# A gated recurrence with a ternary feed-forward: Bm's products move to slot 7, two blocks of y to slot 6

## What is computed

```python
def step(carry, xs):
    r, state = carry
    qt, kt, vt = xs                       # kt = vt = ctx, qt = layernorm(x)
    r = decay * r + kt * vt
    retained = (qt * r).reshape(B, D)
    inp = retained @ Wi.T + bi
    gate = sigmoid(inp @ Wg.T + bg)
    blended = gate * state + (1.0 - gate) * inp
    state = tanh(blended @ A.T + inp @ Bm.T)
    out = state @ Wo.T + bo
    return (r, state), out
x = x + tanh(g_xattn) * outs
h = relu(layernorm(x) @ Wq1.T + b1)       # 256 -> 1024, Wq1, Wq2 ternary
x = x + tanh(g_ffn) * (h @ Wq2.T + b2)    # 1024 -> 256
```

## The kernel before

| slot | TensorE behind the step |
|---|---|
| 0 | hidden 0 (8 matmuls), transposes of xh1 (4), output 0 (6) |
| 1 | hidden 1, output 1 |
| 2 | hidden 2, `inp_product` (12) |
| 3 | hidden 3, y blocks 0, 1 (4 each) |
| 4 | y 2, 3, `gate_product` (12) |
| 5 | y 4, 5, transposes of xh2 (4) |
| 6 | y 6, 7, `from_inp` (12) |
| 7 | `from_rest` (12) |

## Time and profile before

### The profile page before, as it was taken

How to read it: one execution, slowest core, us unless ns; L and a number is a source line. 1 busy time by engine, 2 the same in 40 slices (tenths; PEclk the granted TensorE clock), 3 DMA queues, 4 the chain that set the end, 5 groups by cost and what they waited for, 6 DMA issues and landing times. The chain is left out here.

```text
span 317.4 us, 10191 instructions
## 1 busy us (share of the span) xinstructions
PE 304.0 (96%) x3818; PEld 278.1 (88%) x3818; DVE 283.4 (89%) x816; ACT 236.9 (75%) x556; POOL 78.5 (25%) x138
## 2 busy tenths in 40 slices
PE   7889979999999999999999999999999999999995
PEld 5767868899999999999999999999999999997784
DVE  5889899999999999999999999999999998968763
ACT  4585548787778787887877787878877777857693
POOL 2021133241231323141412313231414121141230
PEclk9999999999999999999999999999999999999999
DMA  7903405123444435251533434441514314171321
GB/s 283 404 11 101 100 35 82 58 49 50 134 69 136 66 118 84 71 113 33 134 45 132 66 132 66 127 71 59 126 32 135 45 66 66 69 101 36 68 33 66
DMA packets 19399, 29.16 MB, mean 92 GB/s; under 512 B 1840, under 2 KB 10288, under 8 KB 19120
## 3 DMA queue, kind: packets, MB, share of 16 engines
q0 software_dynamic: 8720, 8.39, 18.5%
q1 hardware_dynamic: 10224, 19.93, 17.9%
q10 hardware_dynamic: 432, 0.53, 0.5%
HBM read 16.26 MB, written 4.19 MB: 64 GB/s over the span
## 5 line engine op out<-in xcount | busy, mean ns | idle before, releaser
L467 ACT ACTIVATE state<-pre_ps,sc 128x64 f32<-128x64 f32 x128 | 40.0, 312 | 51.2 <-PE pre_ps L1077 51.0
L457 ACT ACTIVATE hid<-hid_ps,b_s 128x256 f32<-128x256 f32 x120 | 50.2, 470 | 11.4 <-PE hid_ps L1116 9.7
L1116 PE MATMUL hid_ps<-xt_lo,w_q 128*128 128x256 f16 x240 | 55.5, 272 | 0.0
L1128 PE MATMUL y_ps<-w_q,h_lo 128*128 128x256 bf16 x240 | 55.5, 272 | 0.0
L1116 PE MATMUL hid_ps<-xt_hi,w_q 128*128 128x256 f16 x240 | 55.5, 272 | 0.0
L1128 PE MATMUL y_ps<-w_q,h_hi 128*128 128x256 bf16 x240 | 55.5, 272 | 0.0
L1071 PE MATMUL pre_ps<-m_hi,a_hi 128*128 128x32 f16 x508 | 42.6, 179 | 4.5 <-DVE m_hi L681 4.3
L732 DVE TENSOR_TENSOR h_lo<-hid,h_hi 128x512 f16<-128x512 f32 x60 | 41.3, 688 | 3.1 <-ACT h_hi L463 1.4
L1071 PEld LDWEIGHTS pre_ps<-m_hi,a_hi 128*128 128x128 f16 x508 | 33.7, 96 | 10.7 <-DVE m_hi L681 6.5
L1071 PE MATMUL pre_ps<-m_hi,a_lo 128*128 128x32 f16 x508 | 41.5, 177 | 0.0
L463 ACT CAST h_hi<-hid 128x512 f16<-128x512 f32 x60 | 37.1, 619 | 1.9
(11 more groups left out here) (181 smaller groups left out, 916.5 us busy)
## 6 DMA issues: line engine op xcount, KB each, us to landing
x_norm<-x_in SPq DMA_DIRECT2D x16, 256.0 KB, 2.7
cx<-ctx_in SPq DMA_DIRECT2D x16, 256.0 KB, 3.1
x_res<-x_in SPq DMA_DIRECT2D x16, 256.0 KB, 3.3
x_res<-bo_g POOLq DMA_DIRECT2D x16, 256.0 KB, 4.8
x<-b_g POOLq DMA_DIRECT2D x15, 256.0 KB, 3.9
y_out<-y SPq DMA_DIRECT2D x15, 256.0 KB, 2.0
w_raw<-w_in SPq DMA_DIRECT2D x2, 1024.0 KB, 8.4
wsq<-wsq_in SPq DMA_DIRECT2D x3, 256.0 KB, 5.1
```

The lines of the kernel that those rows point to most:

```text
L457: last = nc.scalar.activation(hid[:, p % 2, u, :], hid_ps[p % 2][:, u * N:(u + 1) * N], ACT.Relu, bias=b1_s[:, 2 * p + u:2 * p + u + 1], s ...
L467: nc.scalar.activation(state[:, q[1] % 2, :, step_cols(j)], pre_ps[q[1] % 2][:, :].rearrange("p (k n) -> p k n", k=K)[:, :, step_cols(j)], ...
L1116: last = nc.tensor.matmul(hid_ps[p % 2][:, u * N:(u + 1) * N], w1_q[:, k, cut], v[:, par, k, :], start=n == 0, stop=n == len(terms) - 1)
L1128: last = nc.tensor.matmul(y_ps[:, t * D:(t + 1) * D], h[:, f, t * P:(t + 1) * P], w2_q[:, f, :], start=f == 0 and t == 0 and h is h_hi, st ...
```

## The change

Three places in TensorE's list are edited; no other engine's program changes. y's blocks 2 and 3 leave slot 4 (with the wait that they had in body 2) and go to the head of slot 6's list, so that the order of the blocks is now 0, 1, 4, 5, 2, 3, 6, 7. Both calls of `from_inp` leave slot 6 and stand in slot 7 directly ahead of `from_rest`.

```diff
--- before.py
+++ after.py
@@ -1247,15 +1247,10 @@
                         output_product(attend, j)
                     if j == 2 and project:
                         inp_product(project)
-                    if j == 4 and ffn:
-                        if peeled == 2:
-                            pe.wait_ge(dve_prep, done[f"ternary{QUARTERS + 1}"])
-                        y_product(ffn, 2)
-                        y_product(ffn, 3)
                     if j == 4 and project:
                         gate_product(project)
                     if ffn:
-                        for f in {3: (0, 1), 5: (4, 5), 6: (6, 7)}.get(j, ()):
+                        for f in {3: (0, 1), 5: (4, 5), 6: (2, 3, 6, 7)}.get(j, ()):
                             if peeled == 2 and f % 2 == 0:
                                 pe.wait_ge(dve_prep, done[f"ternary{QUARTERS + f // 2}"])
                             y_product(ffn, f)
@@ -1264,10 +1259,9 @@
                     if j == 6 and peeled == NC - 1:
                         end_output(0)
                     if project:
-                        if j == 6:
+                        if j == 7:
                             from_inp(project, 0)
                             from_inp(project, 1)
-                        if j == 7:
                             from_rest(project)
                     if peeled == 0 and j == 2:
```

## The result

| | before | after |
|---|---|---|
| median of 6 runs each, us | 320.44 | 329.62 |
| lowest, highest | 319.57, 321.32 | 327.86, 330.22 |
| the profiled execution | 319.58 | 327.86 |
| its span | 317.4 | 325.7 |

The ratio is 1.0278, 95% interval 1.0252 to 1.0304: the change makes the kernel slower by 2.8%, 9.2 us by the medians and 8.3 us by the two profiled executions. 329.0 was predicted, 8.4 us by the sum in the profiled execution's terms.

The account below looks back on a forecast made before the run. TensorE's list of products was taken to set the chunk's period, with VectorE's lead deciding stalls. 6.9 (chunks 2 to 13) + 0.3 (chunk 14) + 0.9 (chunk 1) + 0.3 (chunk 15) = 8.4 us gave 329.0, range 327 to 331.

Parts of the forecast that it names:

- TensorE alone, +0.06 a chunk: Slots 4, 6 and 7 behind their steps: 6.15 us against 6.09 before, if VectorE kept up.
- the turn: Slot 4, first float32 product behind a step: the next starts after 0.21 instead of 0.12, costing 0.09 us.
- G(5) stays 9.83 behind E(0): VectorE's m_hi feeding step 5 stays 9.83 us behind the first product after step 0, despite reaching slot 0 earlier.
- The rival in which that lead is carried to step 7: Step 7: VectorE's extra lead removes the stalls, leaving 0.8 us, 321.7; chance 5%.
- Steps 5, 6, 7: Odd chunks: late m_hi (G) delays the first product after each step (E); period 18.03 against 17.40, +0.63 us.
- a stall of 0.18 and one of 0.37: TensorE held by late m_hi from VectorE: 0.18 us at step 6 and 0.37 at step 7.
- the prediction's signs: TensorE idle before step 7's first matmul, some 0.35 us a chunk, released by m_hi; period about 18.0.
- The head's 0.9: Chunk 1: slot 6 loses 1.41 us of products to slot 7, partly regained in chunk 2; 0.9 taken from 0.5 to 1.4.
- the end's 0.3: Chunk 15: slot 6 gets 0.87 us more, residual needs its end product; 0.3 us taken from 0 to 0.87.
- That rival (chance 8%, 4 us): Chunk 1 idling drops TensorE's clock to 1.2 GHz, or inp_hi holds the gate's products: 4 us more, 333; chance 8%.
- Total work decides: Whole kernel: the larger busy time a chunk sets the period whatever the order; no change, 319.6 to 320.9; chance 3%.
- Half the stall: Stalls at steps 6 and 7 overlap otherwise, or the head's 0.9 is hidden: 4.2 us, 325; chance 10%.

Follow-up runs that it names:

- the covered turn: Kernel before, with the last of the 4 matmuls of y's block 7 moved behind slot 7's step, directly ahead of from_rest: 319.12 us, ratio 0.9979.
- the moved h_lo: Changed kernel with VectorE's last h_lo of the chunk moved from slot 5 to slot 6, behind the gated state: 329.16 us, ratio 1.0306.
- the kernels with another order of VectorE: Changed kernel with VectorE's last h_lo moved to slot 6 (329.16 us), its scan moved to the end of slot 7 (323.01), or both (320.30).
- both edits of VectorE's order: Changed kernel with VectorE's scan moved from slot 6 to slot 7 and the last h_lo from slot 5 to slot 6: 320.30 us, ratio 1.0013.

## Why the prediction was right, point by point

**TensorE alone, +0.06 a chunk.** Right. Behind the steps, slots 4, 5 and 7 take 1.51, 1.31 and 2.92 in chunk 7 after (1.50, 1.30 and 2.91 were worked out), the turn included. The trace after shows 0.21 for the turn in slot 4 again. The Trainium skill ("TensorE: Matmul & The Clock Gate", Step-by-step: what each phase is for) says that the next weights load while a matmul runs. The traces agree behind a product of 256 columns (the covered turn, 0.22 with that product in it), and not directly behind the step, whose matmuls are 0.03 us apart.

**G(5) stays 9.83 behind E(0).** Right, and the point that the forecast hung on: 157.88 - 148.06 = 9.82. h_lo of slot 1 is at 150.65, 2.59 behind E(0), where it was 2.60, although VectorE reached slot 0 with 1.2 us more lead, and h_hi's cast starts 1.94 behind E(0) in both traces. The rival in which that lead is carried to step 7 failed here.

**Steps 5, 6, 7.** Worked out: G(6) 11.61, G(7) 14.03, E(7) 14.81 behind E(0), next E(0) 18.03. Measured: 11.60, 14.00, 14.77, 18.00. The even chunks: +0.54 (18.04 against 17.50), +0.52 worked out. As the moved h_lo showed, the words "a stall of 0.18 and one of 0.37" were a loose account: the sum is right since E(7) is G(7) + 0.77 whatever happens at step 6. Nor is it all idle time before step 7's first matmul, as the prediction's signs had it: 0.13 us stand there and 0.20 inside the step.

**The sum.** Chunks 2 to 13: 6.9 worked out. By the traces E(0) of chunk 2 is late by 1.43 and that of chunk 14 by 7.70 (266.36 to 274.06); less the 0.91 that remains of the head, 6.8. The head's 0.9 is 0.91, chunk 14's 0.3 is 0.28 (7.70 to 7.98, chunk 15's E(0) at 283.75 and 291.73), the end's 0.3 is 8.3 - 7.98 = 0.3. Sum 8.3, by a span of 325.7 against 317.4.

The head and the end were picked out of ranges (0.5 to 1.4, and 0 to 0.87), so that both came out to a tenth is in part luck. For the end the reason was wrong, too. The prediction had the residual wait for the end product issued in slot 6. In the trace after it is y that VectorE waits for, whose blocks had moved:

```profile
305.50 0.75 DVE L740 SCALAR_TENSOR_TENSOR y<-y_ps,gate_sc,x 128x512 f32<-128x512 f32 x1 [0.19 <-PE y_ps L1128]
```

The residual stands right behind it, 14.61 us behind chunk 15's E(0), where it stood 14.33. With h_lo of slot 5 moved, TensorE keeping its new order, it is at 14.33 again.

**From the sum to the median.** Here the numbers came out right for a reason in part not given, which is luck. The median of before fell from 320.89 to 320.44 with three more runs, and that of after, 329.62, holds a dip of the clock in most runs that the forecast had put down to a rival. That rival (chance 8%, 4 us) named a place where such a dip was seen, but mis-sized it: 1.5 us, and not in every run. Its other half, inp_hi holding the gate's products, didn't happen: the gate's product starts directly at 156.82.

**The rivals.** "Total work decides" is refuted by the kernels with another order of VectorE: same work, 320.3 to 329.2. "Half the stall" would have given periods near 17.7, and they are 18.0.

## What to carry to other kernels

In a recurrence with filler between its steps, write down for each step how much earlier its operand is ready than the engine that takes it arrives, on both sides; moving filler away from ahead of a step spends that lead, and busy shares (96% and 89% here) don't show it. Work moved to behind the tightest step needn't pay back: here VectorE's lead of 1.9 us at step 0 was down to 0.59 at step 2, for it has to wait for what each step and TensorE's products give it. When an order on one engine is changed, look which instruction on the other engine now stands in the slot that got shorter: moving the scan alone gave back 4.9 of 8.3 us.

## What the runs showed that was not expected

Float32 products of one run of 24 did not always have the same pitch. In the kernel with both edits of VectorE's order, chunk 7, these two starts are seven pitches apart:

```profile
160.67 0.28 PE L1027 MATMUL pre_ps<-rest_hi,aw_hi 128*128 128x256 f32 x1
...
161.46 0.28 PE L1027 MATMUL pre_ps<-rest_hi,aw_lo 128*128 128x256 f32 x1
```

and in chunk 8 these:

```profile
178.19 0.28 PE L1027 MATMUL pre_ps<-rest_hi,aw_hi 128*128 128x256 f32 x1
...
179.01 0.28 PE L1027 MATMUL pre_ps<-rest_hi,aw_lo 128*128 128x256 f32 x1
```

That is 0.113 us each in the first and 0.117 in the second, at full granted clock; slot 7 behind its step takes 2.81 in chunks 5, 7, 9, 11 and 13 and 2.91 or 2.92 in the others. In the changed kernel it took 2.91 or 2.92 in all chunks from 2 to 13 but one (2.81 in chunk 11). No run here tells what decides between the two.

And most runs of the changed kernel hold a dip of the clock. The one seen in its trace came behind a stretch of chunk 1 in which TensorE was busy 1.38 us of 3: some 3 us of products at 1.2 GHz, 1.5 us of time. Other kernels had such dips at other places, so that the stretch makes them more frequent is likely and not shown. In the two profiled executions without a dip the change costs 8.3 us; the medians, 9.2 apart, hold some of the dip.
